# The second half of a layer-norm chain moved between stages of a two-layer decoder, and one layer norm folded into its projections

## The reference

```python
def _layernorm(x, axis=-1, eps=1e-05):
    m = jnp.mean(x, axis=axis, keepdims=True)
    v = jnp.var(x, axis=axis, keepdims=True)
    return (x - m) / jnp.sqrt(v + eps)
...
x = x + _L0_attn_ref(_layernorm(x), ...)               # chunked delta rule with decays
x = x + _L0_xattn_ref(_layernorm(x), ctx_1024, ...)    # attention 0, tanh layers
x = x + _L0_ffn_ref(_layernorm(x), ...)                # 4 experts, top 2, own norm at its end
x = x + _L1_attn_ref(_layernorm(x), ...)               # attention 1
x = x + _L1_xattn_ref(_layernorm(x), ctx_1024, ...)    # attention 2, causal
x = x + _L1_ffn_ref(_layernorm(x), ...)                # 8 experts, top 2
```

```python
def _L1_attn_ref(x, Wc_down, Wq_up, Wkv_up, Wc_proj):
    latent = x @ Wc_down                               # 256 -> 128
    q = (latent @ Wq_up).reshape(Bsz, Tlen, N_HEAD, HEAD_DIM)
    kv = latent @ Wkv_up                               # one key and one value for all 16 heads
    k, v = (kv[..., :HEAD_DIM], kv[..., HEAD_DIM:])
    att = jnp.einsum('bthd,bsd->bhts', q, k) * scale   # causal softmax follows
```

## Time and profile before

| | us |
|---|---|
| median of 3 runs | 5926.64 (5919.98 to 5928.34) |
| the profiled execution, its own time | 5926.71 |
| its span, first to last instruction | 5925.0 |
| one iteration, from DVE's first L1692 to the next | 348.3 to 351.5 |

### The profile page before, as it was taken

One profiled execution on the slowest core, in us unless ns is written; L12 is line 12 of the kernel. 1 busy time (PEld: TensorE's weight loads), 2 busy tenths in 40 slices (PEclk: granted clock), 3 DMA queues, 4 the chain that ended last, 5 costly groups with the idle time before them and its releaser, 6 DMA issues.

```text
span 5925.0 us, 105693 instructions
## 1 busy us (share of the span) xinstructions
PE 4872.4 (82%) x28358; PEld 3170.5 (54%) x28358; DVE 4148.9 (70%) x11598; ACT 2292.7 (39%) x4416; POOL 3821.2 (64%) x10626
## 2 busy tenths in 40 slices
PE   1078888988888888888888888888888889888888
PEld 0055655646565565656546565564656556465655
DVE  5857676776767667676766767676676767667686
ACT  0033434444334444433444443444434344443344
POOL 1168485775848577584866848476684857758475
PEclk7589999999999999999999999998999999999999
DMA  3000000000000000000000000000000000000000
GB/s 84 5 12 8 19 1 23 5 8 20 8 20 1 16 12 8 20 5 23 1 12 16 8 20 1 23 5 8 20 8 20 1 23 5 8 20 8 12 1 15
DMA packets 61969, 79.06 MB, mean 13 GB/s; under 512 B 11168, under 2 KB 53808, under 8 KB 61232
## 3 DMA queue, kind: packets, MB, share of 16 engines
q1 hardware_dynamic: 52784, 62.42, 3.2%
q10 hardware_dynamic: 8448, 8.39, 0.4%
HBM read 45.04 MB, written 8.46 MB: 9 GB/s over the span
## 4 chain that ended last, share of the span: by engine, by line
PE 52%; DVE 25%; issue 10%; ACT 7%; POOL 3%; DMA 2%; SPq 1%; DVEq 0%; POOLq 0%; ACTq 0%
PE bank L1058 6%; PE bank L1072 6%; PE bank L1151 5%; PE bank L1082 4%; PE bank L982 3%; PE bank L989 3%; PE bank L1184 3%; PE bank L1104 2%; PE bank L1064 2%; PE bank L1091 2%; POOL arena L560 2%; DVE arena L1877 2%; ACT arena L756 1%; PE bank L1169 1%; ACT arena L743 1%
## 5 line engine op out<-in xcount | busy, mean ns | idle before, releaser
L1742 DVE TENSOR_REDUCE smax<-bank 128x4 f32<-128x512 f32 x768 | 525.2, 684 | 161.1 <-PE bank L1064 121.1
L739 ACT ACTIVATE arena<-bank 128x512 f32<-128x512 f32 x768 | 455.6, 593 | 426.0 <-PE bank L1072 424.4
L1746 DVE TENSOR_TENSOR arena<-bank,smax 128x512 f32<-128x512 f32 x768 | 531.2, 692 | 26.4
L1072 PE MATMUL bank<-ident,arena 128*128 128x128 f32 x3072 | 484.6, 280 | 34.1 <-ACT arena L732 19.4
L1151 PE MATMUL bank<-w,arena 128*128 128x512 f32 x1024 | 499.7, 620 | 14.0 <-DVE arena L1686 14.0
L1058 PE MATMUL bank<-arena 64*128 64x512 f32 x1536 | 452.3, 667 | 64.8 <-DVE arena L1916 27.2
L560 POOL TENSOR_TENSOR arena<-arena,levmask 128x512 f32<-128x512 f32 x192 | 256.8, 1353 | 362.1 <-PE bank L982 237.4
L1082 PE MATMUL bank<-arena 128*32 128x128 f32 x6144 | 327.5, 284 | 190.8 <-ACT arena L743 190.8
L1072 PEld LDWEIGHTS bank<-ident,arena 128*128 128x128 f32 x3072 | 346.3, 141 | 228.6 <-ACT arena L732 90.0
L1184 PE MATMUL bank<-w,arena 128*128 128x256 f32 x2048 | 454.2, 380 | 13.9 <-ACT arena L793 13.9
L494 POOL TENSOR_TENSOR arena<-arena 128x1024 f32<-128x1024 f32 x17 | 32.2, 1896 | 645.9 <-DVE y_nat L1533 645.8
(11 more groups left out here) (427 smaller groups left out, 11906.5 us busy)
## 6 DMA issues: line engine op xcount, KB each, us to landing
arena<-in_x_dram SPq DMA_DIRECT2D x35, 512.0 KB, 3.6
xn_next<-arena SPq DMA_DIRECT2D x17, 512.0 KB, 2.9
arena<-cum_dram SPq DMA_DIRECT2D x17, 512.0 KB, 3.7
arena<-in_ctx_dram SPq DMA_DIRECT2D x16, 512.0 KB, 3.6
out_dram<-arena ACTq DMA_DIRECT2D x16, 512.0 KB, 3.2
xn<-xn_next SPq DMA_DIRECT2D x15, 512.0 KB, 2.9
w<-in_L_ffn_w_dram SPq DMA_DIRECT2D x8, 512.0 KB
w<-in_L_ffn_w_dram SPq DMA_DIRECT2D x1, 1024.0 KB
```

What stands on the lines that cost most here:

```text
L739: act.activation(PT[:, v % 2], bank[3 + v % 2][:, :].rearrange("p (h q) -> p h q", h=QH), ACT.Copy).then_inc(S["pt"], 1)
L1072: ins = tr(bank[3 + v % 2][:, j * P:(j + 1) * P], Ssb[:, v % 4, j, :], ident[:, :])
L1742: dve.tensor_reduce(smax[:, u, :], sc, AX, ALU.max).then_inc(S["s_max"], 1)
L1746: dve.tensor_tensor(Ssb[:, u % 4], sc, smax[:, u, :].unsqueeze(2).broadcast_to([P, QH, P]), ALU.subtract).then_inc(S["s_sub"], 1)
```

## The change

- Norm 3 is no longer applied to the rows. PE transposes `xres` itself, half by half (`residual_features(3, 4, MIX_FILL, 2)`), with the filler (now 14 matmuls) between the halves. The mean is taken out by centring the columns of `Wcd` once, ahead of the loop. The reciprocal root goes, per query token, into the scale of the exponential (as attention 2 has it already), and per key token into keys and values: keys and values are made token by token in one small matmul each sequence, DVE multiplies keys (`k_nat`, repeated for eight heads) and values by `rstd`, and PE transposes `k_nat`. The factor `SCALE` goes into the copy of the queries. `Wkr` is gone.
- `exact_quotient(1)` goes from the slot e = 2 to the slot e = 3. `exact_rest(1)` and the rest of the half m = 1 go into attention 1: one of the eight instructions of `exact_rest(1)` behind every second subtraction, the two subtractions (`exact_difference`) ahead of the division of the third sequence, and the last two instructions, with `x_norm`, ahead of the division of the fourth. The half m = 1 has a scratch place of its own for this.
- POOL's wait for `x_norm` now stands ahead of `chain_products(3)`; the wait for `xT_dve` there is gone.

```diff
-        quo, quo_p, quo_e, quo_h, quo_l = (unit(u, lo, 2 * D).rearrange("p (b d) -> p b d", d=D) for u, lo in ((21, 0), (21, 512), (22, 0), (22, 512), (1, 512)))
+        quotients = [[unit(u, lo, 2 * D).rearrange("p (b d) -> p b d", d=D) for u, lo in places]
+                     for places in (((21, 0), (21, 512), (22, 0), (22, 512), (1, 512)), ((5, 0), (5, 512), (6, 0), (4, 512), (16, 512)))]
...
+                chain_links(pool, link, 2, 2, 16)
                 pool.wait_ge(x_norm, nth(it, 1, 1, 2))
-                chain_links(pool, link, 2, 2, 16)
-                pool.wait_ge(S["xT_dve"], at(it, "xT_dve", 4))
                 chain_products(pool, link, src, 3)
...
-                            if a_no == 2:
+                            if a_no > 0:
                                 if v == 0:
-                                    act.wait_ge(S["hl_fix"], at(it, "hl_fix", 6 * 4 + 6))
+                                    act.wait_ge(S["hl_fix"], at(it, "hl_fix", 6 * (a_no + 2) + 6))
...
-                half_rstd(3)
                 xT_copy(3)
+                half_rstd(3, 0, 1)
                 act.wait_ge(S["lat_psum"], at(it, "lat_psum", 1))
                 act.activation(latT, bank[2][:, :], ACT.Copy).then_inc(S["lat"], 1)
+                half_rstd(3, 1, 2)
...
+            for c in range(C):
+                ins = mm(bank[3][:, D:D + P], ones[:, :], Wcd[:, c, :], start=(c == 0), stop=(c == C - 1))
...
+                            if a_no == 1 and v == 0:
+                                pe.wait_ge(S["v"], at(it, "v", 4))
...
-                keep_busy(MIX_FILL, 2)
-                to_features(3)
+                residual_features(3, 4, MIX_FILL, 2)
                 xT_ready(3)
                 for c in range(C):
                     ins = mm(bank[2][:, :], Wcd[:, c, :], xT[:, c, :], start=(c == 0), stop=(c == C - 1))
                 ins.then_inc(S["lat_psum"], 1)
                 pe.wait_ge(S["lat"], at(it, "lat", 1))
-                mm(bank[3][:, :], Wkr[:, :, :].rearrange("p a b -> p (a b)"), latT, start=True, stop=True).then_inc(S["k_psum"], 1)
+                for g in range(G):
+                    ins = mm(bank[7][:, g * 2 * HD:(g + 1) * 2 * HD], latT[:, g * P:(g + 1) * P], Wkv[:, :], start=True, stop=True)
+                ins.then_inc(S["v_psum"], 1)
                 for c in range(C):
                     mm(bank[4 + c][:, :], Wqu[:, c * P:(c + 1) * P], latT, start=True, stop=True).then_inc(S["q_psum"], 1)
+                pe.wait_ge(S["k_rows"], at(it, "k_rows", 1))
                 for g in range(G):
-                    ins = mm(bank[2][:, g * HD:(g + 1) * HD], latT[:, g * P:(g + 1) * P], Wkv[:, HD:2 * HD], start=True, stop=True)
-                ins.then_inc(S["v_psum"], 1)
+                    ins = tr(bank[3][:, g * P:(g + 1) * P], k_nat[:, g].rearrange("p a b -> p (a b)"), ident[:, :])
+                ins.then_inc(S["k_psum"], 1)
                 pe.wait_ge(S["q"], at(it, "q", 4))
-                pe.wait_ge(S["v"], at(it, "v", 4))
                 attention(1, True, 1, Wcp)
...
+                link(dve.scalar_tensor_tensor(out=Wcd[:, c, :], in0=bank[3][:, D:D + P], scalar=-1.0 / D, in1=Wcd[:, c, :], op0=ALU.mult, op1=ALU.add))
...
-            def exact_rest(m):
+            def exact_rest(m, part, b):
+                quo, quo_p, quo_e, quo_h, quo_l = quotients[m]
+                q, n, last, op = ((quo_h, 7, quo_p, SUB), (quo_h, 8, quo_e, ADD), (quo_l, 7, quo_e, ADD), (quo_l, 8, quo_e, ADD))[part]
+                step(stt(out=quo_e[:, b, :], in0=q[:, b, :], scalar=row[:, n, 2 * m + b:2 * m + b + 1], in1=last[:, b, :], op0=MUL, op1=op))
+            def exact_difference(m):
+                quo, quo_p, quo_e, quo_h, quo_l = quotients[m]
+                xr = x_in[:, 2 * m:2 * m + 2, :]
+                step(tt(xr, xr, quo_p, SUB))
+                step(tt(xr, xr, quo_e, SUB))
+            def exact_last(m):
+                quo = quotients[m][0]
                 xr = x_in[:, 2 * m:2 * m + 2, :]
                 one = lambda n, b: row[:, n, 2 * m + b:2 * m + b + 1]
-                by_row(lambda b: stt(out=quo_e[:, b, :], in0=quo_h[:, b, :], scalar=one(7, b), in1=quo_p[:, b, :], op0=MUL, op1=SUB))
-                by_row(lambda b: stt(out=quo_e[:, b, :], in0=quo_h[:, b, :], scalar=one(8, b), in1=quo_e[:, b, :], op0=MUL, op1=ADD))
-                by_row(lambda b: stt(out=quo_e[:, b, :], in0=quo_l[:, b, :], scalar=one(7, b), in1=quo_e[:, b, :], op0=MUL, op1=ADD))
-                by_row(lambda b: stt(out=quo_e[:, b, :], in0=quo_l[:, b, :], scalar=one(8, b), in1=quo_e[:, b, :], op0=MUL, op1=ADD))
-            def exact_norm(m):
-                xr = x_in[:, 2 * m:2 * m + 2, :]
-                one = lambda n, b: row[:, n, 2 * m + b:2 * m + b + 1]
-                step(tt(xr, xr, quo_p, SUB))
-                step(tt(xr, xr, quo_e, SUB))
                 if m == 0:
...
+                            if a_no == 1 and u % 2:
+                                exact_rest(1, u // 4, u // 2 % 2)
                         if u >= 6 and (u - 6) % 4 == 3 and (u - 6) // 4 < G:
                             b = (u - 6) // 4
+                            if a_no == 1 and b == 2:
+                                exact_difference(1)
+                            if a_no == 1 and b == 3:
+                                exact_last(1)
...
                     if e == 1:
                         exact_quotient(0)
-                        exact_rest(0)
+                        for part in range(4):
+                            for b in range(2):
+                                exact_rest(0, part, b)
                         key_limit(it, 1)
                     if e == 2:
-                        exact_norm(0)
-                        exact_quotient(1)
+                        exact_difference(0)
+                        exact_last(0)
                     if e == 3:
                         key_rows(it, 1, xn_next)
-                        exact_rest(1)
-                        exact_norm(1)
-                layer_norm(3, xres, lambda m: mixture_norm(m) if m else None)
+                        exact_quotient(1)
+                mixture_norm(1)
+                half_stats(3, 0, xres)
                 xT_copy(3)
+                half_stats(3, 1, xres)
+                half_root(3, 0)
+                half_root(3, 1)
                 beta_rows(it, 1)
+                wait("v_psum", 3)
+                kv = bank[7][:, 0:G * 2 * HD].rearrange("p (g d) -> p g d", d=2 * HD)
+                dve.tensor_tensor(k_nat, kv[:, :, 0:HD].unsqueeze(2).broadcast_to([P, G, HPC, HD]),
+                                  rstd[:, :].unsqueeze(2).unsqueeze(3).broadcast_to([P, G, HPC, HD]), ALU.mult).then_inc(S["k_rows"], 1)
                 for c in range(C):
                     wait("q_psum", 2 + c + 1)
-                    dve.tensor_copy(QT[:, c, :], bank[4 + c][:, :]).then_inc(S["q"], 1)
-                wait("v_psum", 3)
+                    dve.tensor_scalar(QT[:, c, :], bank[4 + c][:, :], SCALE, None, ALU.mult).then_inc(S["q"], 1)
                 for m in range(2):
                     for g in (2 * m, 2 * m + 1):
-                        ins = dve.tensor_copy(V2[:, g, :, 0:HD], bank[2][:, g * HD:(g + 1) * HD].unsqueeze(1).broadcast_to([P, NH, HD]))
+                        ins = dve.tensor_scalar(V2[:, g, :, 0:HD], kv[:, g, HD:2 * HD].unsqueeze(1).broadcast_to([P, NH, HD]), rstd[:, g:g + 1], None, ALU.mult)
                     ins.then_inc(S["v"], 1)
                 attention(1)
...
-MIX_FILL = 16
+MIX_FILL = 14
```

30 lines of the change are left out of this document (16 added, 14 removed).

## The result

The changed kernel takes 6002.7 us (median of 4 runs, 5999.6 to 6006.4) against 5927.5 for the kernel before: a ratio of 1.0128, with a 95% interval of 1.0113 to 1.0143. It is slower by 75 us. The sign was forecast, and the time lies inside the range of 5900 to 6020, but the forecast's own loss was 33 us. The profiled execution has a span of 5997.9 us.

The account below looks back on a forecast made before the run. No one engine bounds everywhere; gains ahead are given back when DVE waits 10.5 us for POOL's `au`. +0.1 - 0.5 + 2.5 = +2.1 us for each of 16 iterations, 33 us, plus 0.5 setup, on 5926.7: 5960 us, range 5900 to 6020.

Parts of the forecast that it names:

- The sign: Whole kernel: slower than before, chance 0.60; faster by over 0.2% 0.22, within 0.2% 0.18.
- the price of the setup: Ahead of the loop: two more small products on DVE, 0.5 us once.
- The expert loop: End of the expert loop: DVE stops delaying the last expert's weighting; mixture ends 5.1 (A) and 5.7 us (B) sooner.
- From the experts to attention 1: Mixture's end to latent 1.9 us, gaining 4.4; latent to first maximum 12.1, A loses 0.3, B gains 2.2.
- the term of 2 us for the half clock: Latent to first maximum of attention 1: one stretch at half clock over latent or queries adds 2 us to 10.1.
- the rival of the clock that holds: PE stays warm before attention 1: -1.6 us an iteration, 5901 us; chance 0.16.
- Inside attention 1: Eight moved steps, 4.2 us in all, mostly fit idle time; attention 1 grows 0.3 us, bounds 0 and 7.
- The steps of the rest: Eight exact-norm steps moved into attention 1, expected hidden; rival that they are not: 7.1 us an iteration, 6040 us, chance 0.15.
- the rival of a wait that does not bind: DVE's wait for `au` in attention 2 does not bind: some 10 us an iteration gained, 5765 us; chance 0.05.
- After the stall: From DVE's wait for `au` on: decay start +0.1, vanished wait for PE -0.5, clock +2.5; +2.1 us an iteration.
- The term of 2.5 us for TensorE's half clock: Behind the stall in attention 2: PE at half clock after idling 11 us delays the second addend 2.5 us, bounds 0 and 5.

Follow-up runs that it names:

- Experiment 4: Changed kernel with GpSimd's wait for the normalised rows moved behind the fourth slice's products: 5845.7 us, ratio 0.9874 to the kernel before.
- experiment 5: Two runs on the changed kernel: GpSimd's mean subtraction held until VectorE's last feature copy, 5998.0 us; 40 filler matmuls in TensorE's wait in the third attention, 6012.0 us.
- 6: Each half of the change alone: folded norm without the moved exact norm, 5894.9 us; moved exact norm on the kernel before, 6054.6 us.
- 7: Changed kernel with GpSimd's wait behind the products and setup two instructions shorter, 5825.3 us; subtraction also moved, 5771.6; then setup four fills longer instead, 5747.5.

## Why the prediction was wrong, and what of it held

The step that failed is the price of the setup; it stands last below, behind the terms in the order of the prediction.

*The expert loop.* Right in kind, too large in size. DVE no longer holds up the last weighting, but the mixture ends at 189.8 us, 3.6 sooner than before and not 5.1 to 5.7; the weightings of the experts ahead of it come up to 2.1 us later than before.

*From the experts to attention 1.* 11.9 us instead of the 14.0 worked out. No run shows the term of 2 us for the half clock: PE was granted 0.98 over this stretch (in the iteration shown above), where it had 0.69 (A) and 0.58 (B), and without the term the chain was forecast at 1.9 + 10.1 = 12.0 us. The stretches, read as in the earlier trace rows, from the mixture's end to the first maximum, in the changed kernel and then before:

```profile
3000.90:3012.80 11.90, 7.53 (x30) 3.60 (x30) 7.81 (x30) 4.48 (x10) 9.53 (x40) 0.98 0.01 2
```

```profile
2966.34:2984.44 18.10, 11.90 (x32) 5.20 (x32) 7.71 (x28) 4.11 (x8) 14.52 (x61) 0.69 0.01 1
3314.95:3335.64 20.69, 14.41 (x32) 6.12 (x32) 7.71 (x27) 4.11 (x8) 16.65 (x70) 0.58 0.00 1
```

So here the rival of the clock that holds was the true one. Attention 1 starts at 201.7, forecast 202, only because this miss and that of the expert loop cancel; that is luck.

*Inside attention 1.* The steps of the rest are hidden: steps 0 to 15 went from 26.5 to 27.1 us. The normalised rows come at 236.3, forecast 235.5, `au` at 292.4, forecast 291.8, and DVE stands 9.8 us, forecast 10.5. Experiment 4 shows this wait to be worth 150 to 157 us, and by that the rival of a wait that does not bind to be what a small reordering reaches.

*After the stall.* Right in sum by luck, wrong in cause. The forecast had +0.1 - 0.5 + 2.5 = +2.1 us; measured +0.6 to the first decay step and +2.5 to the end of the last mixture. The term of 2.5 us for TensorE's half clock was mis-sized: filling the wait kept the clock up and gave nothing (experiment 5), and with the subtraction away 0.6 to 0.8 us of it come to light. In its place GpSimd's 1.9-us subtraction, which the stall moved by 15 us onto DVE's steps in SBUF, holds one of them for 1.58 us. The prediction weighed the rule of the Trainium skill, page "SBUF — State Buffer", section "Who interferes with whom", for the eight steps of the rest and rightly found almost nothing in the row; it did not ask which long GpSimd instruction the stall would move. There the rule holds: the DVE step ended 0.03 us after GpSimd's instruction.

*The setup: the step that failed.* "The setup has two more small products on DVE: 0.5 us." It cost about 40: 46 us on the kernel before, 38 to 46 on the changed one. The prediction priced the two instructions by their duration, and not by the place of the loop behind them: they are run once, but they moved the head of the loop, and DVE then stood 4.8 us instead of 2.4 ahead of the first instruction of every iteration. The rows were in the trace of before: 2.46 and 1.77 us of "issue" ahead of the first two DVE instructions of an iteration. The Trainium skill, page "Runtime: NRT & Kernel Launch", section "Instruction fetch mechanics", says that a taken branch whose target isn't in the engine's current window forces a fetch before execution goes on; the runs agree, with 2.4 us for one fetch and 4.8 us for two. With this term, 16 x 2.4 = 38 us, the forecast would have been 5998. That is near the 6003 measured, but it is not a full account: the 1.8 us ahead of the second instruction went at the same time, and the first row maximum of attention 0 came only 0.7 us sooner for it.

## What to carry to other kernels

A value that another engine needs 56 us of work to use has a due time; when its producer is moved, follow that engine's chain to its reader before counting the gain, and put the consumer's wait only ahead of what really reads it. In a loop of many instructions, read the idle time marked "issue" ahead of the first instructions of an iteration: two instructions more or fewer ahead of the loop moved this kernel by 0.6 to 0.8%, and a few fills that shift the head off the border took it back. Where a stall moves an engine's schedule, look at which long GpSimd instruction lands on which DVE step.

## What the runs showed of the hardware

- A turn of DVE's loop costs 2.4 us of idle time at the best place found, with a further 1.8 us ahead of the second instruction, or 4.8 us ahead of the first, where the loop's head lies across a border. Instructions were fetched twice at each turn, 2.4 us apart, at every place. Delaying a 512 KB store by 4 us took 0.2 us off the idle time, no more.
- A DVE step of 0.17 us took 1.75 us beside a GpSimd subtraction of 1.9 us, with one operand in SBUF (the steps held in experiments 4, 6 and 7 are in part `TENSOR_SCALAR`) as with two.
- TensorE's granted clock fell to 0.50 (1.2 GHz) in windows in which it was busy throughout (6.50 of 6.50 us), behind a wait filled with matmuls as well as behind an empty one. Fillers moved such windows and did not remove all of them; DVE's wait for PE behind them grew from 0.5 to as much as 2.3 us.
